# Two joints of a graph kernel: the order of SyncE's queue after x1, two normalisations on VectorE, and zero products on TensorE

## The reference

```
# layer 0: graph convolution with self loops, residual, layer norm
xp  = x @ W0
out = segment_sum(xp[src] * norm, dst) + b0
x1  = layernorm(x + relu(out))
# layer 1: equivariant edge messages
sj, vj = (x1[:, :C] @ Win_s)[dst], (x1[:, C:] per component @ Win_v)[dst]
W   = (shifted_softplus(rbf @ Wf1 + bf1) @ Wf2 + bf2) * edge_weight
agg = segment_sum(products(sj, vj, Y(vec)) * W, src)
y   = [softplus branch(agg scalars), linear branch(agg vectors)]
return layernorm(x1 + y)
```

## Time and profile before

| | us |
|---|---|
| three runs: median (lowest to highest) | 1079.65 (1079.17 to 1084.14) |
| the profiled execution: its own time | 1074.51 |
| its span in the profile | 1072.7 |
| busy: PE | 920.3 (86%) |
| busy: DVE | 846.7 (79%) |
| busy: ACT | 707.3 (66%) |
| busy: POOL | 652.9 (61%) |

### The profile page before, as it was taken

One profiled execution on the slowest core, in us unless ns is written; L12 is line 12 of the kernel. 1 busy time (PEld: TensorE's weight loads), 2 busy tenths in 40 slices (PEclk: granted clock), 3 DMA queues, 4 the chain that ended last, 5 costly groups with the idle time before them and its releaser, 6 DMA issues.

```text
span 1072.7 us, 17283 instructions
## 1 busy us (share of the span) xinstructions
PE 920.3 (86%) x4812; PEld 743.0 (69%) x4812; DVE 846.7 (79%) x2396; ACT 707.3 (66%) x1642; POOL 652.9 (61%) x945
## 2 busy tenths in 40 slices
PE   7889888999973999999999389999999999915553
PEld 7767777777753888887888268888887888714443
DVE  7688888886824788788889578888888888719997
ACT  4669877777761566666666446666666666638886
POOL 4028888888851566666666345776677676426665
PEclk9989999998995999999999789999999999955555
DMA  9989999999998499999998767999999999688995
GB/s 350 418 274 250 242 237 240 239 240 242 236 224 279 165 341 324 327 315 313 323 323 311 273 187 178 216 206 218 226 217 211 216 228 189 94 220 337 389 400 233
DMA packets 121443, 280.39 MB, mean 261 GB/s; under 512 B 13746, under 2 KB 38342, under 8 KB 121350
## 3 DMA queue, kind: packets, MB, share of 16 engines
q1 hardware_dynamic: 73590, 186.25, 47.9%
q0 software_dynamic: 35280, 82.63, 40.0%
q10 hardware_dynamic: 12480, 10.42, 3.0%
HBM read 132.38 MB, written 146.87 MB: 260 GB/s over the span
## 4 chain that ended last, share of the span: by engine, by line
PE 43%; DVE 11%; DMA 8%; issue 4%; ACT 2%; POOL 1%; SPq 1%; ACTq 0%; DVEq 0%; POOLq 0%
PE bank L1309 8%; PE bank L1357 7%; PE bank L1340 6%; PE bank L1371 5%; DVE stat L1167 4%; PE bank L1313 4%; PE bank L1369 3%; DMA edge_mem<-x 3%; PE bank L1334 3%; PE bank L1300 2%; PE bank L1367 2%; DMA G_mem<-x 2%; PE bank L1346 2%; DVE node_mem L1158 1%; DVE stat L1043 1%
## 5 line engine op out<-in xcount | busy, mean ns | idle before, releaser
L548 POOL DMA_INDIRECT sum<-R_mem,sidx_all x79 | 129.1, 1634 | 85.0 <-DMA sum<-zeros 48.7
L609 POOL DMA_INDIRECT sum<-R_mem,l_sidx x79 | 135.6, 1717 | 45.9 <-issue 21.9
L595 POOL DMA_INDIRECT G_mem<-x_d,dst_i x79 | 77.2, 977 | 90.9 <-PE bank L1344 64.3
L1309 PE MATMUL bank<-G_hi 128*128 128x512 f32 x316 | 131.4, 416 | 0.0
L1309 PE MATMUL bank<-G_lo,G_hi 128*128 128x512 f32 x316 | 124.9, 395 | 0.0
L1225 PE MATMUL bank<-G_hi,M_mem 128*128 128x512 f32 x200 | 86.3, 432 | 7.0 <-ACT R_mem L681 6.4
L1313 PE MATMUL bank<-G_hi,G_lo 128*128 128x512 f32 x316 | 85.3, 392 | 0.0
L1114 DVE SCALAR_TENSOR_TENSOR edge_mem<-edge_mem,Y,bank 128x128 f32<-128x128 f32 x237 | 71.2, 385 | 15.0 <-ACT edge_mem L806 15.0
L1340 PE MATMUL bank<-edge_mem,Winv 128*128 128x512 f32 x158 | 81.8, 600 | 0.1
L1225 PE MATMUL bank<-G_lo,M_mem 128*128 128x512 f32 x200 | 80.5, 402 | 0.0
L1387 PE MATMUL bank<-ident,node_mem 128*128 128x128 f32 x80 | 27.5, 447 | 61.5 <-DVE node_mem L1158 61.5
(11 more groups left out here) (230 smaller groups left out, 2831.5 us busy)
## 6 DMA issues: line engine op xcount, KB each, us to landing
node_mem<-sum SPq DMA_DIRECT2D x41, 512.0 KB, 5.9
filt_d<-node_mem SPq DMA_DIRECT2D x40, 512.0 KB, 4.9
node_mem<-filt_d SPq DMA_DIRECT2D x79, 256.0 KB, 4.9
sum<-zeros SPq DMA_DIRECT2D x33, 512.0 KB, 14.2
G_mem<-x SPq DMA_DIRECT2D x20, 512.0 KB, 6.9
x_d<-node_mem SPq DMA_DIRECT2D x20, 512.0 KB, 3.5
edge_mem<-x SPq DMA_DIRECT2D x19, 512.0 KB, 6.1
x_d<-R_mem SPq DMA_DIRECT2D x19, 512.0 KB, 3.9
```

What stands on the lines that cost most here:

```text
L548: pool.indirect_dma_start(sum0, bass.IndirectOffsetOnAxis(ap=sidx[:, t:t + 1], axis=0), R[t % 8][:, :], None, compute_op=ALU.add).then_inc ...
L595: pool.indirect_dma_start(G3[t % 8][:, :], None, x1_d, bass.IndirectOffsetOnAxis(ap=dst_i[:, t:t + 1], axis=0)) \
L609: pool.indirect_dma_start(sum1, bass.IndirectOffsetOnAxis(ap=l1_sidx[0:n, t:t + 1], axis=0), R3[t % 8][0:n, :], None, compute_op=ALU.add). ...
L1309: pe.matmul(bank[4 + a][:, :], zT_hi[a][:, c * P:(c + 1) * P], w[c][:, :], start=(c == 0 and w is W0h), stop=False)
```

## The change

Four things are edited.

1. `held` and its four semaphores go; its three calls become plain waits.
2. SP: the loads of index rows and filters leave step j = 41 and stand behind the last store of x1, filters first. The stores in `sum1` of pairs 36 to 39 stand behind these loads. The wait for `n_tr` in front of the filter loads goes, since it is passed by then.
3. Tile 77 is normalised by VectorE, like tile 78, and no longer by ScalarE. `n_last` counts two.
4. TensorE multiplies zeros into bank 7 (`keep_clock(7, n)`, n float32 products of 128x128 by 128x512): three once all scatter-adds of edge stage 0 have landed, three once the x1 stores of pairs 38 and 39 have landed, two at step 5 of edge stage 1 ahead of the transposes of tile 1, and one at step 6.

```diff
-                if j == T2 + 1:
-                    for g in range(4):
-                        trow_in(g)
-                    sp_.wait_ge(n_tr, TR)
-                    for t in range(4):
-                        filt_in(t)
                 if j >= 6:
                     i = j - 6
-                    sp_.wait_ge(n_x1, min(2 * i + 2, TR - 1))
-                    if i == T2 - 1:
-                        sp_.wait_ge(n_last, 1)
+                    sp_.wait_ge(n_x1, min(2 * i + 2, TR - 2))
+                    if i >= T2 - 2:
+                        sp_.wait_ge(n_last, i - T2 + 3)
                     sp_.dma_start(layer_pair(x1_d, i, 0, D), in_pair(res2[i % 8], i, 0, D)).then_inc(n_st[i % 8], 16)
-                    for k in ((i,) if i < T2 - 2 else (i - 1, i) if i == T2 - 1 else ()):
-                        sp_.dma_start(layer_pair(sum1, k, C, D), ...).then_inc(rows_st[k % 8], 16)
+                    if i < T2 - 4:
+                        sum1_out(i)
...
             for j in range(T2 + 6):
                 nodes0(j)
+            for t in range(4):
+                filt_in(t)
+            for g in range(4):
+                trow_in(g)
+            for k in range(T2 - 4, T2):
+                sum1_out(k)
...
-            dve.wait_ge(n_root, 2 * K_RSTD)
-            r = res[(TR - 1) % 16]
-            dve.tensor_scalar(r, r, w[:, 5, 0:1], w[:, 6, 0:1], ALU.mult, ALU.add).then_inc(n_last, 1)
+            for t in (TR - 2, TR - 1):
+                g, k, r = t // 2, t % 2, res[t % 16]
+                dve.wait_ge(n_root, K_RSTD * (g - T2 + 3))
+                dve.tensor_scalar(r, r, tiny[g % 4][:, 5, k:k + 1], tiny[g % 4][:, 6, k:k + 1], ALU.mult, ALU.add).then_inc(n_last, 1)
...
+            def keep_clock(b, n):
+                for _ in range(n):
+                    pe.matmul(bank[b][:, :], zeros[:, 0:P], zeros[:, 0:512], start=True, stop=True)
...
             ins.then_inc(s_pairs, 1)
+            pe.wait_ge(e_scat, 16 * TR)
+            keep_clock(7, 3)
...
             pe.wait_ge(s_const, 19)
+            for u in (6, 7):
+                pe.wait_ge(n_st[u], 16 * (T2 // 8))
+            keep_clock(7, 3)
 
             def edges1(s, u):
+                if s in (5, 6):
+                    keep_clock(7, 7 - s)
```

More of the change, by code:

```diff
@@ L377, in build @@
         rows_st = [sem(f"rows_st{i}") for i in range(8)]
[L379 to L387, removed]
         NZ = 8
@@ L473, in nodes0, with sum1_out @@
                         x_in(j)
-                if j == T2 + 1:
-                    for g in range(4):
-                        trow_in(g)
-                    sp_.wait_ge(n_tr, TR)
-                    for t in range(4):
-                        filt_in(t)
                 if j >= 6:
                     i = j - 6
-                    sp_.wait_ge(n_x1, min(2 * i + 2, TR - 1))
-                    if i == T2 - 1:
-                        sp_.wait_ge(n_last, 1)
+                    sp_.wait_ge(n_x1, min(2 * i + 2, TR - 2))
+                    if i >= T2 - 2:
+                        sp_.wait_ge(n_last, i - T2 + 3)
                     sp_.dma_start(layer_pair(x1_d, i, 0, D), in_pair(res2[i % 8], i, 0, D)).then_inc(n_st[i % 8], 16)
-                    for k in ((i,) if i < T2 - 2 else (i - 1, i) if i == T2 - 1 else ()):
-                        sp_.dma_start(layer_pair(sum1, k, C, D), in_pair(res2[k % 8], k, C, D)).then_inc(rows_st[k % 8], 16)
+                    if i < T2 - 4:
+                        sum1_out(i)
+            def sum1_out(k):
+                sp_.dma_start(layer_pair(sum1, k, C, D), in_pair(res2[k % 8], k, C, D)).then_inc(rows_st[k % 8], 16)
             for j in range(T2 + 6):
                 nodes0(j)
+            for t in range(4):
[4 more added lines that the diff above has]
+                sum1_out(k)
             for s in range(4, TR):
@@ L565, in nodes0 @@
                     st.mark(pool.tensor_scalar(w[:, 7, :], mean, -1.0, None, ALU.mult))
-                    held(pool, n_rs, 2 * (g + 1))
+                    pool.wait_ge(n_rs, 2 * (g + 1))
                     st.mark(pool.tensor_tensor(w[:, 3, :], w[:, 2, :], w[:, 2, :], ALU.mult))
@@ L569, in nodes0 @@
                     st.mark(pool.tensor_tensor(w[:, 4, :], w[:, 3, :], w[:, 0, :], ALU.mult))
-                    held(pool, n_rstd, st.reached())
+                    pool.wait_ge(n_rstd, st.reached())
                     st.mark(pool.tensor_scalar(w[:, 3, :], w[:, 4, :], -0.5, 1.5, ALU.mult, ALU.add))
@@ L776, in nodes0 @@
                     r = res[t8 % 16]
-                    if t8 < TR - 1:
+                    if t8 < TR - 2:
                         act.activation(r, r, ACT.Identity, bias=tiny[b][:, 6, k:k + 1], scale=tiny[b][:, 5, k:k + 1]).then_inc(n_x1, 1)
@@ L780, in nodes0 @@
                     t9 = s - 11
-                    if t9 < TR - 1:
+                    if t9 < TR - 2:
                         act.wait_ge(n_x1, t9 + 1)
                     else:
-                        act.wait_ge(n_last, 1)
+                        act.wait_ge(n_last, t9 - TR + 3)
                     act.copy(xs1[t9 // 2][:, t9 % 2 * C:(t9 % 2 + 1) * C], res[t9 % 16][:, 0:C]).then_inc(n_keep, 1)
@@ L828, in edges1 @@
                     t, a = s - 2, (u - 2) % 8
-                    held(act, f_gather[a], 16 * (turn(t, a, 8) + 1))
+                    act.wait_ge(f_gather[a], 16 * (turn(t, a, 8) + 1))
                     wait(act, f_tr, t - 3)
```

## The result

The changed kernel takes 1086.9 us (median of 12 runs, 1085.15 to 1091.51), the kernel before 1079.38 (12 runs beside them): ratio 1.0076, 95% interval 1.0062 to 1.009. It is slower, by 7.5 us, where 1082.8 (1075 to 1086.5) was forecast. The profiled execution took 1087.56, its span is 1085.7.

What follows compares the result with a forecast made beforehand. TensorE was taken to bound both long stages, except at two joints. First joint -1.5, ScalarE's later start +2.9 and second-joint zeros +1.75 gave +3.15 us: 1079.65 becomes 1082.8, range 1075 to 1086.5.

Steps and rivals of the forecast that it cites:

- `held`: Three calls turned into plain waits: they pass a Python integer, so the instructions are the same, 0 us.
- Tile 77 on VectorE: End of node stage 0: VectorE finishes tile 77 sooner, so pair 39's x1 store is issued 0.3 us earlier.
- Joint 1: Edge stage 0 to node stage 0: three zero products raise TensorE's clock sooner, -1.5 us.
- x1 lands sooner: End of node stage 0: x1 complete at 608.75 instead of 611.8, 3.0 us earlier; first gather issued at 609.55.
- Issue of the last deferred store: SP's queue behind x1: after 8.0 us of DMA issues, the last store in `sum1` goes out at about 613.5.
- Landing of that store: Start of edge stage 1: lands at 618.9, between 616.3 and 621.5, and sets ScalarE's start, +2.9 us.
- Zeros at joint 2: Node stage 0 to edge stage 1: first three hidden, those at steps 5 and 6 run with clock down, +1.75 us.
- Sum: Whole kernel: -1.5 + 2.9 + 1.75 = +3.15 us, giving 1082.8 on the median.
- Rival B: Start of edge stage 1: even DMA sharing, last store in `sum1` lands at 621.5; +5.75 us, 1085.4; chance 0.2.
- Rival A: Start of edge stage 1: deferred stores land before the gather, TensorE is warm; -5.95 us, 1073.7; chance 0.15.
- Rival C: Start of edge stage 1: first three zeros raise the clock, still up at 620.3; +0.05 us, 1079.7; chance 0.15.
- D: Rival at joint 1: transposes start 1.0 us later and no clock rises sooner; total +5.65 us, 1085.3; chance 0.08.

Runs made afterwards that it cites:

- zeros1: The kernel before plus only the three zero products once edge stage 0's scatter-adds have landed; ratio 0.9986 to the kernel before.
- order: The changed kernel without any zero products, keeping SP's new order and tile 77 on VectorE; ratio 1.0083 to the kernel before.
- rowslast: The changed kernel with SP's loads and stores behind x1 ordered filters, stores in `sum1`, index rows; ratio 1.0013 to the kernel before.
- after: The changed kernel as first measured and profiled; ratio 1.0076 to the kernel before.
- again: The changed kernel, unedited, measured and traced once more; ratio 1.0052 to the kernel before.
- late: The changed kernel with ScalarE's four `rows_st` waits moved from the head of edge stage 1 to its first write into `R_mem`; ratio 0.9998 to the kernel before.
- sumfirst: The changed kernel with the four stores in `sum1` directly behind x1, ahead of filters and index rows, ScalarE's wait unmoved; ratio 0.9997 to the kernel before.
- zeros2: The kernel before plus only the zero products after the x1 stores and at steps 5 and 6 of edge stage 1; ratio 0.9983 to the kernel before.
- both: The kernel before with all the change's zero products and nothing else; ratio 0.9971 to the kernel before.
- early: The changed kernel with index rows loaded before node stage 0, filters at step 41, ScalarE's wait at its first `R_mem` write; ratio 0.9955 to the kernel before.
- early3: The kernel called early, without the zero products at steps 5 and 6; ratio 0.9959 to the kernel before.

## Why the prediction was wrong

Its mechanism was right, its size was not. It named line 791's wait, said that its cover of 2.8 us is gone, that x1 lands 3 us sooner and that nobody can use it. By its own steps:

- *`held`*: 0, not tested by itself. *Tile 77 on VectorE*, put at 0.3, was run only together with the order.
- *Joint 1*: -1.5 forecast, 1.4 by J1, 1.5 by the ratio of `zeros1`. Right. (The 1.5 used 3.39 us for the eight slow products; the 3.21 of rows 2 give 1.4.)
- *x1 lands sooner*: first gather 5.34 after M forecast (609.55 less 604.21), 5.62 measured. Right.
- *Issue of the last deferred store*: 9.3 after M forecast (613.5 less 604.21), 9.0 measured (616.88 less 607.87). Right.
- *Landing of that store*: this is the step that failed. Forecast 14.7 after M, with 17.3 as the upper bound; measured 20.0 (627.85 less 607.87). ScalarE's start was put at +2.9; it is +8.3, also in `order`. The upper bound was sized by bytes at a full 0.41 MB/us. Two things are wrong with that. From 613 to 618 only 1.25 MB moved, where 2.05 could have (344 + 316 + 274 + 101 + 218 GB/s, a microsecond each): 2.0 us. With the index rows moved back, in `rowslast`, the same stretch after M moved 1.70 MB, so about half of this goes with them; the cause of the rest stays open. And the middle was taken, while in fact everything that the gathers brought (eight of 256 KB, 2.1 MB) was drained before the last store landed: 3.08 + 2.10 = 5.18 MB at 0.41 are 12.6 us, with 2.0 for the slow stretch 14.6, and x1 had landed 15.1 before 627.85; the last 0.5 us are not accounted for.
- *Zeros at joint 2*: +1.75 forecast, +0.15 and +0.65 measured (E in after and again). The first zeros' clock was lost in the wait, as forecast. After tile 0 both steps were shorter than I put them: tile 1 came 3.83 and 4.34 after tile 0 where 4.75 was forecast, tile 2 came 2.52 and 2.51 after tile 1 where 3.2 was. In after the clock rose during the two zeros of step 5 (their four records took 2.86, not 3.42); in `again` they took 3.37, and it rose near their end.
- *Sum*: -1.4 + 8.3 + 0.15 to 0.65 = 7.1 to 7.6, a ratio of 1.0065 to 1.0070. Measured 1.0076 and 1.0052, whose intervals both hold it. Rival B had the place and the sign (+5.75), and again the landing too early, at 17.3.

Rival A needed 700 GB/s and would have failed even then: `late` and `sumfirst`, in which no store holds ScalarE, are no faster than before, because the gather itself is slowed. Rival C's clock held through tile 2 where the wait behind the zeros was short, as in `zeros2`, `both` and `early` (0.2 to 1.3 us). D did not happen.

## What to carry to other kernels

Before work is moved behind a transfer that gates the next stage, list every wait on the work that is moved. Count what other queues will bring while the moved work drains. Here four stores were also a buffer release for ScalarE, and 2.8 us of cover turned into 8.3 us of loss. A deferred DMA isn't free when the next stage's first reads use the same engines: what can go early (the index rows had a buffer of their own all the time) should go early, not late. Products that raise the clock paid here when real work followed them within 1.3 us, and nothing when it came 3 us or more later.

## What the runs showed of the hardware that was not expected

- Loads that copy one row of up to 1.5 KB to all 128 partitions seem to cost more than their bytes: about 1.2 us for four of them (`rowslast` against after), and with them in the queue the engines were 0.85 busy for 179 GB/s in before, against 0.96 for 341 in `early` without them.
- A deferred transfer is delayed by what other queues bring in the meantime: 2.10 MB of gathers went by before the last store in `sum1` had landed, 5 us at 0.41 MB/us.
- A gather of 256 KB landed in 3.4 us in a quiet queue, 4.3 beside 1.38 MB of stores, 6.4 behind stores and filters, and 7.0 behind filters and index rows.
- The clock was down after 2.3 us without work in `early3`, still up after 2.97 in `sumfirst`, where it fell a microsecond later with TensorE busy, and before it fell about 4 us after TensorE's last product; one figure for it will not do.
- Single executions differ in unchanged parts: 6.5 us at the start in one of fourteen traces, and 253.0 to 257.7 us for the same stretch of node stage 0. A difference of two spans must be cut at fixed points before it is given to an edit.
